# One stream of quads through two 16-head attentions: a written event list, two quads of lag, and another split of the work over the engines

## The reference, cut to what matters

```python
q, k, v = (x @ W.T + b for each)            # 16 heads of 8
dot = einsum('bhqd,bhkd->bhqk', q, k)
# layer 1 (aa): dot = where(causal, dot, -inf) / sqrt(128)
# layer 3 (ab): no mask, dot / sqrt(8); x is turned by RoPE before the projections
out = einsum('bhqk,bhkd->bhqd', softmax(dot), v)
return out.reshape(b, t, 128) @ Wo.T + bo
```

## Time and profile before

| | us | how to read it |
|---|---|---|
| median of the runs | 2,516.8 | three runs |
| span of the profiled execution | 2,520.3 | the rows below are from this one |
| TensorE busy | 1,994.8 | pipelined matmuls overlap, so busy is not full use |
| VectorE busy | 1,683.3 | |
| ScalarE busy | 850.6 | |
| GpSimd busy | 502.1 | |
| layer `aa`, from the first maximum to the last residual | 62.4 to 568.3 | starts of the quads from VectorE's rows |
| layer `ab`, the same | 671.5 to 1,239.9 | |
| DMA | 63 MB, 14% of 16 engines | nearly all of it in packets of 1 KB, in the two attentions |

### The profile page before, as it was taken

The page is one execution under the profiler, slowest core; times in us unless marked ns, Lnnn a source line. Parts: engine busy times, 40 slices in busy tenths (PEclk is TensorE's granted clock), DMA queues, the critical chain, the costliest instruction groups (busy, mean ns, idle before and its releaser), DMA issues. The chain is left out here.

```text
span 2520.3 us, 37035 instructions
## 1 busy us (share of the span) xinstructions
PE 1994.8 (79%) x12009; PEld 1174.1 (47%) x12009; DVE 1683.3 (67%) x3783; ACT 850.6 (34%) x1324; POOL 502.1 (20%) x421
## 2 busy tenths in 40 slices
PE   1688887885388998899669999999999856668566
PEld 0244444443122222222237777777778534445344
DVE  1666666646388877887257776677666469945897
ACT  0033343353025545556542222322232322223122
POOL 1111111003221111110120000000000446620566
PEclk9788888896569989999789999999999978879787
DMA  6333333200323222221000000000000000000000
GB/s 151 61 54 56 53 53 52 52 2 2 50 52 52 52 52 52 43 46 15 1 0 1 1 1 1 1 1 2 1 1 1 1 0 1 0 1 0 5 13 17
DMA packets 71728, 63.01 MB, mean 25 GB/s; under 512 B 11528, under 2 KB 69384, under 8 KB 71560
## 3 DMA queue, kind: packets, MB, share of 16 engines
q1 hardware_dynamic: 71560, 60.87, 13.7%
HBM read 45.51 MB, written 15.20 MB: 24 GB/s over the span
## 5 line engine op out<-in xcount | busy, mean ns | idle before, releaser
L488 DVE TENSOR_REDUCE ab_M<-ps 128x1 f32<-128x512 f32 x512 | 331.3, 686 | 91.8 <-PE ps L372 76.4
L332 ACT ACTIVATE ab_probs<-ps 128x1024 f32<-128x1024 f32 x256 | 260.3, 1024 | 250.9 <-PE ps L399 248.9
L488 DVE TENSOR_REDUCE aa_M<-ps 128x1 f32<-128x384 f32 (+3 forms) x352 | 216.3, 639 | 157.6 <-PE ps L377 144.9
L372 PE MATMUL ps<-ab_KS,ab_QS 72*128 72x512 bf16 x512 | 217.4, 430 | 74.6 <-DVE ab_M L488 40.0
L332 ACT ACTIVATE aa_probs<-ps 128x1024 f32<-128x1024 f32 (+1 forms) x192 | 168.4, 882 | 284.3 <-PE ps L402 282.2
L372 PE MATMUL ps<-aa_KS,aa_QS 72*128 72x384 bf16 (+3 forms) x512 | 156.1, 340 | 121.3 <-DMA aa_KS<-aa_parts_dram 89.5
L1439 PE MATMUL ps<-gate_up,fp_xT 128*128 128x352 f32 x256 | 127.9, 665 | 91.3 <-DVE fp_xh L1481 90.3
L372 PEld LDWEIGHTS ps<-ab_KS,ab_QS 72*128 72x128 bf16 x512 | 51.3, 100 | 263.1 <-DVE ab_M L488 205.3
L416 PE MATMUL ps<-ab_probs,ab_V 128*9 128x512 f32 x1024 | 145.6, 643 | 21.3 <-ACT ab_probs L332 15.9
L399 PE MATMUL ps<-ab_QS,ab_KS 74*128 74x512 bf16 x512 | 160.1, 399 | 0.5 <-ACT ab_probs L332 0.5
L372 PEld LDWEIGHTS ps<-aa_KS,aa_QS 72*128 72x128 bf16 x512 | 54.5, 107 | 192.2 <-DMA aa_KS<-aa_parts_dram 65.3
(11 more groups left out here) (286 smaller groups left out, 3981.3 us busy)
## 6 DMA issues: line engine op xcount, KB each, us to landing
aa_QS<-aa_parts_dram SPq DMA_DIRECT2D x144, 64.0 KB
aa_KS<-aa_parts_dram SPq DMA_DIRECT2D x144, 64.0 KB
ab_QS<-ab_parts_dram SPq DMA_DIRECT2D x144, 64.0 KB
ab_KS<-ab_parts_dram SPq DMA_DIRECT2D x144, 64.0 KB
aa_parts_dram<-aa_splitq SPq DMA_DIRECT2D x24, 128.0 KB, 1.8
aa_parts_dram<-aa_splitk SPq DMA_DIRECT2D x24, 128.0 KB, 1.8
ab_parts_dram<-ab_splitq SPq DMA_DIRECT2D x24, 128.0 KB, 1.8
ab_parts_dram<-ab_splitk SPq DMA_DIRECT2D x24, 128.0 KB, 1.8
```

Of the source, the lines that this page charges most:

```text
L332: act.activation(v(probs[r][:]), v(src), ACT.Exp, scale=scale).then_inc(scores_free, 1)
L372: last = pe.matmul(ps[:, FIRST + b, o * stride:o * stride + width], QS[par][0:ROWS, h, qt * P:(qt + 1) * P], KS[par][0:ROWS, h, 0:width], ...
L488: v.tensor_reduce(M[:, heads[0]:heads[-1] + 1, qt], src, AX.X, ALU.max).then_inc(max_free, 1)
```

## The change

- `walk` and its loop are replaced by a list of events, `attention_order`: each event has a time in units of a quad, the list is sorted by time, and every engine executes its own events in that order, fully unrolled. Quad g of the stream (g = 4n + q) has its first pass at g, `nm` at g + 1.30, and its second pass from g + 2 on (`LAG`). Sorted, this gives for a middle sequence, with quads counted from the start of the sequence before: on GpSimd "mask of unit 1, split of q, nm of quad 0, masks of units 2 and 3, split of k, masks of units 4 and 5" in quad 1; on TensorE "first 1, q, first 2, sum, scores 1, first 3, turn of nm" in the same quad in `aa`, and the first unit of a quad, then the scores of the quad two before. On SyncE: nm of quad 1, store, half 0, nm of quad 2, half 1, nm of quad 3.
- The negation of the maxima goes from VectorE to GpSimd (`negate`, two operations, with the maxima in two buffers), the split of k from VectorE to GpSimd (but for the first sequence), the copies of nm and of the sums from VectorE to ScalarE, V is written by ScalarE instead of by VectorE and GpSimd. The bias of v is folded into the output bias by one matmul at the start.
- In `aa` the mask of the second pass is no longer a matmul (L402 is gone): GpSimd clears the diagonal blocks of the exponentials (`clear_future`), and `sum_keys` waits for it. The mask of the first pass stays a matmul, and its maxima stay plain reductions.
- `sum_keys` works in pieces of at most 256 query columns: 6 in `aa`, 8 in `ab`.
- The two shift rows of `QS` hold nm with another sign in the second row, and the constant rows of `KS` are 1 and -1.

```diff
-    first, second = score_units(causal)
-    N1, N2 = len(first), len(second)
+    first, second, pieces = score_units(causal)
+    N1, N2, N3 = len(first), len(second), len(pieces)
...
+def attention_order(items, causal):
+
+    slots = QUADS * items
+    found = []
+
+    def at(time, what, n, q, i=0):
+        found.append((time, len(found), what, n, q, i))
+
+    if causal:
+        f_at = [u / 11 for u in range(11)]
+        s_at = [0.04, 0.20, 0.36, 0.50, 0.66, 0.82]
+        sum_at = [0.46, 0.55, 0.77, 0.87, 1.05, 1.19]
+        copy_at = 1.23
+    else:
+        f_at = [u / 16 for u in range(16)]
+        s_at = [(i + 0.25) / 8 for i in range(8)]
+        sum_at = [at / 4 for at in (1.875, 2.11, 2.375, 2.875, 3.375, 3.875, 4.375, 4.63)]
+        copy_at = 1.20
+    at(-4, "bias", 0, 0)
+    for n in range(items):
+        t0 = QUADS * (n - 1)
+        for t in range(4):
+            at(t0 + 0.02 + 0.09 * t, "stat", n, 0, t)
+        at(t0 + 0.39, "spread", n, 0)
+        for t in range(4):
+            at(t0 + 0.53 + 0.06 * t, "norm", n, 0, t)
+        at(t0 + 0.74, "turn", n, 0)
+        at(t0 + 1.03, "xT", n, 0)
+        at(t0 + 1.17, "q", n, 0)
+        at(t0 + 1.20, "split", n, 0, 0)
+        at(t0 + 1.55, "k", n, 0)
+        at(t0 + 1.58, "split", n, 0, 1)
+        at(t0 + 3.12, "v", n, 0)
+        at(t0 + 2.33, "store", n, 0)
+        at(t0 + 2.50, "half", n, 0, 0)
+        at(t0 + 3.40, "half", n, 0, 1)
+        for q in range(QUADS):
+            g = QUADS * n + q
+            for u, t in enumerate(f_at):
+                at(g + t, "first", n, q, u)
+            at(g + 1.30, "nm", n, q)
+            for i, t in enumerate(s_at):
+                at(g + LAG + t, "scores", n, q, i)
+            for i, t in enumerate(sum_at):
+                at(g + LAG + t, "sum", n, q, i)
+            at(g + LAG + copy_at, "copy", n, q)
+            at(g + LAG + 1.44, "tail", n, q)
+        at(QUADS * n + 3 + LAG + 1.62, "oT", n, 0)
+        at(QUADS * n + 3 + LAG + 1.82, "y", n, 0)
+    return [event[2:] for event in sorted(found)]
...
-            eng.wait_ge(misc_free, m + 1)
-            wait(eng, stack_loaded[1], 16 * STACK_DMAS * n)
-            eng.tensor_tensor(parts[0][:], src[:], core["zeros"][:], ALU.add)
-        if i == 1:
-            eng.tensor_tensor(rest[a][:], src[:], parts[0][:], ALU.subtract)
-        if i == 2:
-            eng.tensor_tensor(parts[1][:], rest[a][:], core["zeros"][:], ALU.add)
-        if i == 3:
-            eng.tensor_tensor(parts[2][:], rest[a][:], parts[1][:], ALU.subtract)
-        drained = eng.drain()
-        if i == 3:
-            drained.then_inc(split_ready, 1)
+        eng.wait_ge(misc_free, uses_of_misc("qk"[a], n))
+        if n:
+            eng.wait_ge(parts_stored, 16 * 2 * SPLITS * n)
+        eng.tensor_tensor(parts[0][:], src[:], core["zeros"][:], ALU.add)
+        eng.drain()
+        eng.tensor_tensor(rest[a][:], src[:], parts[0][:], ALU.subtract)
+        eng.drain()
+        eng.tensor_tensor(parts[1][:], rest[a][:], core["zeros"][:], ALU.add)
+        eng.drain()
+        eng.tensor_tensor(parts[2][:], rest[a][:], parts[1][:], ALU.subtract).then_inc(split_ready[a], 1)
...
+        def split_part(n, q, gq, a):
+            if n or a == 0:
+                split_into(g, a, n)
+
+        def negate(n, q, gq, i):
+
+            g.wait_ge(max_free, N1 * (gq + 1))
+            if gq:
+                g.wait_ge(misc_full, uses_of_misc("nm", (gq - 1) // QUADS, (gq - 1) % QUADS))
+            g.tensor_scalar(nm[:, 0], M[gq % 2][:], -1.0, None, ALU.mult)
+            g.drain()
+            g.tensor_tensor(nm[:, 1], M[gq % 2][:], nm[:, 0], ALU.add).then_inc(nm_ready, 1)
+
+        def clear_future(n, q, gq, i):
+
+            _, heads, width, stride = second[i]
+            u = N2 * gq + i
+            diagonal = probs[u % 4][:].rearrange("p (h c) -> p h c", c=stride)[:, 0:len(heads), 0:P]
+            g.wait_ge(scores_free, u + 1)
+            g.affine_select(out=diagonal, in_=diagonal, compare_op=ALU.is_ge, fill=0.0, base=0,
+                            pattern=[[0, len(heads)], [1, P]], channel_multiplier=-1).then_inc(probs_masked, 1)
+
+        does = {"spread": root, "turn": turn, "split": split_part, "nm": negate}
+        if causal:
+            does["scores"] = clear_future
+        walk(does)
...
+        def store(n, q, gq, i):
+
+            if n:
+                sp.wait_ge(stack_loaded[1], 16 * STACK_DMAS * n)
...
+        def send_nm(n, q, gq, i):
+
+            sp.wait_ge(misc_free, uses_of_misc("nm", n, q))
+            sp.dma_start(nm_dram[q], nmT[q][:]).then_inc(nm_stored, 16)
+            sp.wait_ge(nm_stored, 16 * (gq + 1))
+            sp.dma_start(QS[n % 2][ROWS:ROWS + SHIFT_ROWS, 4 * q:4 * q + 4],
+                         nm_dram[q].rearrange("(r j t) k -> r j (t k)", r=SHIFT_ROWS, j=4)).then_inc(nm_loaded[q], 16)
+
+        walk({"store": store, "half": stack, "nm": send_nm})
...
+        def take_v(n, q, gq, i):
+
+            act.wait_ge(misc_full, uses_of_misc("v", n))
+            if n > 1:
+                act.wait_ge(sums_ready, N3 * QUADS * (n - 1))
+            act.activation(V[n % 2][:, :, :, 0:DH], misc4.rearrange("p t (h d) -> p t h d", h=HEADS), ACT.Copy)\
+                .then_inc(misc_free, 1)
+
+        def take_nm(n, q, gq, i):
+            act.wait_ge(misc_full, uses_of_misc("nm", n, q))
+            if n:
+                act.wait_ge(nm_loaded[q], 16 * n)
+            act.activation(nmT[q][:], misc.bitcast(BF16)[0:32, 0:P], ACT.Copy).then_inc(misc_free, 1)
...
+        def take_sums(n, q, gq, i):
+
+            act.wait_ge(sums_ready, N3 * (gq + 1))
+            if gq:
+                act.wait_ge(misc_full, uses_of_misc("tail", (gq - 1) // QUADS, (gq - 1) % QUADS))
+            act.activation(C[:].rearrange("p t c -> p (t c)"), ps[:, SUMS, :], ACT.Copy).then_inc(sums_free, 1)
...
-                if causal:
-                    last = pe.matmul(ps[:, bank, c:c + P], core["ident16"][:], core["mask_kq"][:],
-                                     start=False, stop=True)
...
+        def sum_keys(n, q, gq, i):
+
+            kt, lo, hi = pieces[i]
+            pe.wait_ge(probs_masked, N2 * gq + last_unit(kt) + 1)
+            if gq == 0 and i == 0:
+                pe.wait_ge(set_up, 1)
+            if q == 0 and i == 0:
+                pe.wait_ge(misc_free, uses_of_misc("v", n))
+            if gq and i == 0:
+                pe.wait_ge(sums_free, gq)
+            for u in range(N2):
+                at, heads, width, stride = second[u]
+                if at != kt:
+                    continue
                 for o, j in enumerate(heads):
-                    last = pe.matmul(ps[32 * j:32 * j + DH + 1, SUMS, 512 - width:512],
-                                     V[par][:, kt, 4 * hq + j, :],
-                                     probs[(N2 * hq + i) % 4][:, o * stride:o * stride + width],
-                                     start=kt == 0, stop=kt == 3, tile_position=(0, 32 * j))
-            last.then_inc(probs_free, len(mine))
-
-        def tail(n, hq, i, par, m):
-            pe.wait_ge(sums_free, QUADS * n + i + 2)
-            pe.wait_ge(misc_free, m + 1)
+                    c = o * stride + lo - (512 - width)
+                    last = pe.matmul(ps[32 * j:32 * j + DH + 1, SUMS, lo:hi], V[n % 2][:, kt, 4 * q + j, :],
+                                     probs[(N2 * gq + u) % 4][:, c:c + hi - lo],
+                                     start=i == 0, stop=i == N3 - 1, tile_position=(0, 32 * j))
+            last.then_inc(sums_ready, 1)
...
+        def split_part(n, q, gq, a):
+            if n == 0 and a == 1:
+                split_into(v, a, n)
+
+        def maxima(n, q, gq, u):
             qt, heads, width, stride = first[u]
-            b = (N1 * (QUADS * par + hq) + u) % 2
-            src = ps[:, FIRST + b, :].rearrange("p (h c) -> p h c", c=stride)[:, 0:len(heads), 0:width]
-            v.wait_ge(max_ready, N1 * (QUADS * n + hq) + u + 1)
-            v.tensor_reduce(M[:, heads[0]:heads[-1] + 1, qt], src, AX.X, ALU.max).then_inc(max_free, 1)
-            if u == N1 - 1:
-
-                v.drain()
-                v.tensor_scalar(nm[:, 0], M[:], -1.0, None, ALU.mult)
-                v.drain()
-                v.scalar_tensor_tensor(nm[:, 1], M[:], -1.0, nm[:, 0], ALU.mult, ALU.subtract)\
-                    .then_inc(nm_ready, 1)
-                v.drain()
-
-        def nm_back(n, hq, i, par, m):
-            v.wait_ge(misc_full, m + 1)
-            v.tensor_copy(nmT[i][:], misc.bitcast(BF16)[0:32, 0:P]).then_inc(misc_free, 1)
-            v.drain().then_inc(nmT_ready, 1)
-
-        def sums_out(n, hq, i, par, m):
-
-            v.wait_ge(probs_free, N2 * (QUADS * n + i + 1) + 4)
-            v.tensor_copy(C[:].rearrange("p t c -> p (t c)"), ps[:, SUMS, :]).then_inc(sums_free, 1)
-
-        def tail(n, hq, i, par, m):
-            v.wait_ge(misc_full, m + 1)
+            U = N1 * gq + u
```

(5 more changed lines are left out.)

348 lines of the change are left out of this document (156 added, 192 removed).

## The result

The changed kernel takes 2,652.7 us (median of 4 runs, 2,648.9 to 2,659.5), the kernel before 2,516.3 in the same comparison: a ratio of 1.055 (1.051 to 1.058), 5.5% slower. The forecast was 2,559, with a range to 2,640. The profiled execution's span is 2,653.2 us against 2,520.3: 133 us more, where +42 was predicted.

The account below looks back on a forecast made before the run. TensorE, busy most of both attentions, waited for the stack in `aa` and for maxima in `ab`. Middle sequences (+45 in `aa`, +1 in `ab`), clock +27 and ends -31 gave +42 on 2,516.8: 2,559 us, range 2,455 to 2,640.

Parts of the forecast that it names:

- A: First pass waits for the stack of split parts: 6 us per sequence in `aa`, 1.5 in `ab`.
- B: Scores wait for the nm load queued behind the stack's second half: 8 us per sequence in `aa`, 3.5 in `ab`.
- C: TensorE's turn of nm waits for GpSimd's negation behind the q split: 7 us per sequence in `aa`, 5.5 in `ab`.
- D: In `aa` alone, the sum waits for a GpSimd mask behind the k split: 3.5 us per sequence.
- TensorE's work with waits for maxima: Period of a middle sequence if free of stalls: 44 us in `aa`, 56 in `ab`.
- the clock term: Low TensorE clock behind the waits: 3 us per sequence in `aa`, 1.5 in `ab` (0 to 7 each).
- 12 us or more: Sign in the trace: SP's nm store and load behind the second half this far apart, TensorE waiting for the load.
- the 28 us up to the landing of the stack: Least length of quads 2 and 3 with the stack's transfers, against 22 us of work in `aa`, 28 in `ab`.
- Ends: Fill, last sequence and drain: drains -16 us in `aa`, -23 in `ab`; with the starts -12 and -19.
- Rival 3: Each of four waits brings back 1.2 GHz: periods near 77 and 74 us, 2,628 us in all; chance 0.13.
- Rival 1: B, C and D are hidden, the stream runs free: periods 50 and 57.5 us, 2,367 in all; chance 0.17.
- Rival 2: Shifts arrive in time, only GpSimd's order bites: periods 61 and 63, clock +14, 2,480 us in all; chance 0.15.

Follow-up runs that it names:

- e10_again: e10 run once more, unchanged, beside e13: 2,416.0 us, 0.962 of the kernel before.
- e10: Changed kernel, negation earlier, second stack half later, splits in four spread pieces, input turn and tail shifted, second-pass masks back on TensorE: 2,427.3 us, 0.962 of before.
- e5: Changed kernel with only the q split moved, to just behind the negation: 2,557.1 us, 1.018 of the kernel before.
- e13: e10 with the second half of the stack back ahead of the next nm in SyncE's list: 2,499.4 us, 0.992 of the kernel before.
- e3: Changed kernel with the second-pass masks of `aa` back on TensorE as matmuls, order kept: 2,584.9 us, 1.029 of the kernel before.
- e8: e4 with n useless GpSimd operations ahead of the negation in the third quad of sequence n of `ab`: 2,595.7 us, one run.
- e4: Changed kernel with the negation ahead of mask and q split, and the stack's second half issued behind the next nm: 2,494.5 us, 0.993 of before.
- e9: As e10, but with the second-pass masks of `aa` left on GpSimd: 2,472.6 us, 0.978 of the kernel before.
- e12: Kernel before, with seven useless float32 matmuls ahead of TensorE's wait for the stack in `aa`: 2,505.3 us, 0.993 of the kernel before.
- e11: Changed kernel with 34, 10 or 26 useless matmuls ahead of TensorE's wait for the negation: 2,651.2 us, 1.051 of the kernel before.

## Why the prediction was wrong

The direction was right, and the time 94 us too low. By its own terms, per middle sequence:

| | `aa` predicted | `aa` after | `ab` predicted | `ab` after |
|---|---|---|---|---|
| A, stack | 6 | 0 | 1.5 | 0.3 |
| B, load of nm | 8 | 0.8 | 3.5 | 0.9 |
| C, negation behind the split | 7 | 7.2 | 5.5 | 5.8 |
| negation behind a mask, in the other quads | none | 5.5 | | |
| D, sum behind a mask | 3.5 | 2.8 | | |
| turn behind RoPE's input | | | none | 1.2 |
| TensorE's work with waits for maxima, and the clock | 44 + 3 | 60.7 | 56 + 1.5 | 65.3 |
| sum | 71.5 | 77.0 | 68.0 | 73.5 |

The last terms are what is left of the period; 5.5 is (76.1 - 43) / 6. The waits alone came out at 16.3 and 8.2 us, where 24.5 and 10.5 were forecast; the loss is in the line below them.

**The failed step is the clock term.** I took 3 and 1.5 us per sequence. By an estimate from e10_again it was 17.4 and 6.3. That run gives the work by itself: in `ab` 60.0 us at clock 1.00, less 2.0 of waits, plus 1.0 of them for maxima, is 59; in `aa` 55.5 less 4.9 of waits, less 3.3 for the clock of 0.94 (at the two levels 12% of 55.5 us are low, and half of that is lost), less 4 for the masks it has on TensorE, is 43.3. So the work was counted right in `aa` (44) and 3 us short in `ab` (56), and 60.7 - 43.3 = 17.4 and 65.3 - 59 = 6.3 us are left for the clock: 17.4 - 3 and 6.3 - 1.5, six times each, is 115 us, more than the whole miss.

The clock records of the traces lead to much the same without e10. Take TensorE's idle time from a period, and half of the time that it was busy at 1.2 GHz, as if all work took twice as long there. What is left is 41.1 to 44.2 us in `aa` for the eight kernels with GpSimd's masks, 46.7 to 47.5 for the five with these masks on TensorE, and 56.1 to 57.3 in `ab` for all thirteen (fillers and the kernel before left out). So periods from 55.5 to 77.0 us differ by waits, clock and these masks, to about 3 us. The halves are 19.6 us in `aa` (39.2 us busy at the low level) and 8.2 in `ab` (16.4) for the changed kernel; by these the clock term was 140 us short.

The reason I gave, that slack behind A and B would hide the low clock, fell with A and B: neither was there. And I priced the low stretch by one row, 6.1 us behind a wait of 6. In the changed kernel, over two sequences of `aa`, the low stretches were 3.4, 6.8, 10.2, 13.7, 23.9, 10.2, 20.5 and 23.9 us long, at waits of 2.0, 3.9, 7.2, 3.0, 2.0, 7.2, 3.0 and 2.0. (The waits of the quads behind a mask alone are 2.0, 1.7 and 2.0 us.) Those at the 7.2 us of wait C lie half inside it, so only 5.2 and 4.9 us of them came behind: for the long wait my row was a fair price. The long stretches stood behind the short waits for masks, which I had given no price of their own, and often the next wait came before one had ended.

The Trainium skill (TensorE: Matmul & The Clock Gate, Why this matters for your kernels) warns of idle gaps between matmul bursts. This case's trace agrees (0.86 before, 0.68 after, in `aa`), and waits of 2.0 us, too, were followed by low clock here. I used the page for the direction only.

**C: right.** 7.2 and 5.8 us where 7 and 5.5 were worked out from the order and the row of the split (10 - 2.4 is 7.6, which I had put down as 7), and e5 shows the cause by taking it away. **What I missed beside it** is that in every quad the mask of unit 1 stands ahead of nm as well. I had written that order out and counted it only where the split follows. It is 5.5 us of wait per sequence. The masks take 0.41 us for two heads and 0.48 on the average of all 192 on the page, less than the 0.5 to 1.2 I took; what costs is waiting for the exponential, with the negation behind it.

**D: right**, 2.8 for 3.5 us.

**B: its mechanism right, its size half, and covered here.** SyncE's pair is 10.6 us apart as forecast (for the "12 us or more" it fell short), and TensorE hardly waits: quads of 19 us on the average instead of 11 leave room. I had set B against quads of full speed and C and D beside it as if independent; the slower quads pay for B. That is shown from the other side only: in e13, where quads are quick, B is 4.0 us of wait and 6.8 of period.

The Trainium skill (DMA: Bandwidth & Descriptors, Queues, rings and completion order) says that on each DMA engine descriptors are consumed in ring order; the 10.1 us in e13 with a half ahead, against 1.3 without one, agree.

**A: wrong.** No wait for the stack in `aa`, and 0.5 us per sequence at most in e10; e3 has 2.4. Nothing speaks against the 28 us up to the landing of the stack, which no run measured by itself, but I set 22 us of work against them, half of 44. A sequence's own work isn't spread evenly: quads 2 and 3 of e10 take 16.4 and 12.9, together 29.3, and so cover the 28.

**Ends.** The two drains are 12.3 and 27.7 us shorter (forecast 16 and 23). The fills and last sequences are 43.8 us longer in place of 8: `aa` +7.9 and +17.7, `ab` +13.1 and +5.1, at clocks of 0.70, 0.73, 0.58 and 0.89. They hold the same waits as the middle, and for them I had kept only B. Of the drains, `aa`'s ran at 0.74 where it had 0.96 before and fell 4 us short of the forecast gain, `ab`'s at 1.00 went 5 beyond it. Other stretches gave 9.3 back.

In sum it is +33 us over the forecast in the middle of each attention, +35 at the ends, -9 elsewhere, which is the miss of 91 us (133 for 42) but for rounding.

**The rivals.** Rival 3 (the clock stays low) is what happened, with periods of 77.0 and 73.5 where it said 77 and 74; I gave it 0.13. Part of this is luck: of the four waits that it builds on, A and B were not there, and the waits behind masks did their work. In `aa` its condition held: 0.68 between levels of 0.5 and 1 is 64% of the time at the low one. In `ab` it did not (0.87, a quarter), and the 74 is right by a mix of a heavier base and C. Its total of 2,628 was 25 short: 35 by the ends, less 9 elsewhere. Rival 1 is not what this kernel does, but e10 comes near it: 55.5 and 60.0 us, against the 50 and 57.5 given. Rival 2 (one chain only: the shifts arrive in time, GpSimd's order bites) is the changed kernel by its waits, B at 0.8 and 0.9 us, C at 7.2 and 5.8. Its periods of 61 and 63 were 16.0 and 10.5 us short, since it too had the clock at 14 us in all and no wait per quad. So the waits are rival 2's and the time is rival 3's.

## What to carry to other kernels

In a written order, price an instruction by all that stands ahead of it on its engine in every repetition, not only where the long one does; a two-operation negation of 0.5 us behind work that waits for another engine cost 5.5% of this kernel, and moving its event by one number gave all of it back. Price TensorE's waits by what they do to the clock, and do so with the next wait in view: many short waits were worse than one long one (24 of 1.9 us and seven for masks in e5: clock 0.73; five of up to 11.1 us in the kernel before: 0.86). When several waits are predicted on one engine, they need not add: here the ones behind GpSimd slowed the stream, and the one for DMA nearly vanished (0.8 us, 4.0 in e13).

## What the runs showed of the hardware

In the middle of `aa` of the changed kernel each of the 21 waits of TensorE of 1.9 us or more that began at full clock was followed by a fall to 1.2 GHz; the waits of 1.9 to 2.0 us by low stretches of 3.4 to 23.9 us. The waits of 1.7 us there all lay in stretches that were low already, so they show nothing. It is no rule: in e5 three waits of 2.0 us were followed by none. In `ab`, waits of 1.1 to 1.5 us stood at full clock in eight places, alone or two close together, and four of these were followed by a fall. Single waits of 1.8, 3.0, 4.2, 5.3, 6.8 and 7.7 us in e8 went with 6.8, 3.4, 13.7, 58.0, 61.4 and 13.7 us at the low level. I had not expected a spread so wide, nor that two executions with the same instructions in `aa` (e4, e8) would differ by 3.4 us per sequence and 0.04 of clock, or in `ab` (e9, e10) by 4.0 and 0.07.

Counting TensorE's busy time at 1.2 GHz at half its length accounts for every period of the thirteen kernels above to about 3 us. Useless matmuls in a wait paid 0.7% where the wait was one and long (e12); in e11 they gave back 8.3 us of clock per sequence of `aa` and 10.1 of waiting, and took 14 themselves.
